# A power of two numbers per partition, moved behind a large sum on GpSimd, in the layers of an attention and feed-forward kernel

## The chip, the cores and the metric

The kernel runs on one core of a Trainium2 chip. A core has five engines, each with a queue of its own that it works off strictly in order: TensorE (PE; its weight loads are listed apart as PEld), VectorE (DVE), ScalarE (ACT), GpSimd (POOL) and SyncE (SP), which here only starts DMAs. Engines wait for one another by semaphores. The metric is the device time of one execution in microseconds; the kernel before took 2054.12 us, the median of three runs (2053.56 to 2055.71).

## The reference

`x` is (1, 2048, 128) in float32. It first goes through an RWKV block with a layer norm, then through six layers of local attention and a gated feed-forward, and a last layer norm. The change lies in the six layers:

```
for i in range(6):
    x = attn_layer(shift_tokens(x), Wqkv[i], ...) + x      # 16 heads of 64, window 32
    x = ffn_layer(shift_tokens(x), ln_g[i], ln_b[i], ...) + x

attn_layer:  q, k, v = split(x @ Wqkv);  q = l2norm(q) * qs;  k = l2norm(k) * ksc
             q = q*cos*scale + rotate_half(q)*sin*scale;  k = k*cos/scale + rotate_half(k)*sin/scale
             out = softmax(8 * q k^T in the window) v;  return out @ Wo
ffn_layer:   mu = mean(x);  var = mean((x-mu)^2);  xn = (x-mu)/sqrt(var + 1e-5) * g + b
             a, gate = split(xn @ W1 + b1);  return a * gelu(gate) @ W2 + b2
```

The power in question is `(var + eps) ** -0.5` of the feed-forward's norm.

## The kernel before

`layers` works in 96 steps of one tile of 128 tokens, 16 tiles in each of six layers, as a software pipeline. In step `s` each engine does a slice of several tiles: the projection, norm and rotation of tile `p = s + 1`, the scores of tile `a = s`, the softmax's rest and the output of tile `b = s - 1`, and, of a pair of tiles some steps back, a slice of the feed-forward. The norm of the feed-forward (`norm`) and its second product (`down`) lie in the odd steps, the first product (`up`) in the even ones. The code is written out by hand for every engine, and that order is the order of the queue. Steps -1 to 6 are unrolled, 88 steps run in a loop of two (an odd one, then an even one), the rest is unrolled again.

The names that matter here:

- `unit[0]`, `unit[1]`: q and k divided by their norms, by DVE, L1152. The inverse root is made by nine small DVE instructions in a chain (`inverse_root`, L88 to L104) from `sums`. All nine read and write SBUF; of them L88, L90, L92, L94 begin the chain. L88 waits for nothing but the sums and its place in the queue behind `heads_out` (L1133), which takes the product of probabilities and values (PE, L1290) out of PSUM.
- POOL's queue for tile `p`: `turns` (the rotary tables of this tile, L993), in odd steps `shift_f` (L1001, L1002), then `shift_a` of the tile after (two copies, L962 and L963), then the first `across` pair (L974, waits for `unit[0]`), `along[0]` (L1008), `rotated[0]` (L982), the second `across` pair (L974, of k), and `rotated[1]` (L982, in `add_turned(1, p)`). `along[1]` is made by DVE (L1210).
- `rotated[1] = along[1] + across[1]`, 128 x 1024 elements, is what PE transposes as `turn<-identity,rotated` in the following step (the second of the two groups at L1223 there). `add_turned` waits for POOL's own `across` through the semaphore `acrossed`, and for DVE's `along[1]`.
- `rstd_f = var_f ** -0.5`, 128 x 2 elements, POOL, L1016. DVE writes `var_f` (L1204) right ahead of its `along[1]`. ACT reads `rstd_f` in the following step, behind its copies to `k_t`, for `rstd_diag` (L1074).
- `proj_a<-w_qkv,shift_a` at L1328: PE's projection of v. It waits for `unit[0]`, since both use the PSUM bank `proj_a`.

Of the kernel before, what the change touches and what calls it, by code (L numbers as in the profile page):

```python
# [65 lines left out]
def after(engine, semaphore, count):  # L66

    if not isinstance(count, int) or count > 0:
        engine.wait_ge(semaphore, count)
# [38 lines left out]
def tile_of(n):  # L108
    return n % TILES


def layer_of(n):
    return n // TILES


def columns(n, count=1):

    return bass.ds(tile_of(n) * TILE + 1, TILE * count)


def columns_before(n, count=1):

    return bass.ds(tile_of(n) * TILE, TILE * count)
# [667 lines left out]
def layers(nc, ctx, given):  # L791
# [12 lines left out]
    with ExitStack() as own:  # L804
# [76 lines left out]
        def halves(buffer):  # L881
            return buffer[:, :, :].rearrange("p h (two e) -> p h two e", two=2)
# [10 lines left out]
        def run(engine, step):  # L893


            for s in range(-1, FIRST):
                step(s, (s - 5) // 2 if s % 2 else (s - 6) // 2, s % 2, alive(s))
            with engine.Fori(0, ROUNDS) as i:
                step(i * 2 + FIRST, i + 1, 1, alive(FIRST + 2))
                step(i * 2 + FIRST + 1, i + 1, 0, alive(FIRST + 3))  # L900
            for s in range(FIRST + 2 * ROUNDS, STEPS + 4):
                step(s, (s - 5) // 2 if s % 2 else (s - 6) // 2, s % 2, alive(s))

        with nc.Block() as block:
# [49 lines left out]
            @block.gpsimd  # L954
            def _(pool):
                pool.wait_ge(tables_in, 48)

                def shift_input(m, odd, pairs_done):

                    after(pool, v_projected, 2 * (m - 1))  # L960
                    pool.wait_ge(xa_ready, XA_BASE + pairs_done)
                    pool.tensor_copy(shift_a[odd][0:64, :], xa[0:64, columns(m)]).then_inc(shifted, 1)  # L962
                    pool.tensor_copy(shift_a[odd][64:128, :], xa[64:128, columns_before(m)]).then_inc(shifted, 1)  # L963
                    pool.wait_ge(shifted, 2 * m + 2)

                def cross(j, p, odd):

                    pool.wait_ge(united[j], p + 1)
                    after(pool, rotated_in[j], p)
                    u, a = halves(unit[j]), halves(across[j])  # L970
                    for half in range(2):
                        table = turns[odd][:, 2 * j + 1, 32 * half:32 * half + 32].unsqueeze(1).broadcast_to(
                            [128, HEADS, 32])
                        pool.tensor_tensor(a[:, :, 1 - half, :], u[:, :, half, :], table, ALU.mult)\  # L974
                            .then_inc(acrossed[j], 1)

                def add_turned(j, p):

                    pool.wait_ge(alonged[j], p + 1)
                    pool.wait_ge(acrossed[j], 2 * p + 2)  # L980
                    after(pool, (q_turned, k_turned)[j], 2 * p)
                    pool.tensor_tensor(rotated[j][:, :, :], along[j][:, :, :], across[j][:, :, :],  # L982
                                       ALU.add).then_inc(rotated_in[j], 1)

                shift_input(0, 0, -XA_BASE + 1)

                def step(s, h, odd, live):
                    p, mine = s + 1, 1 - odd
                    if live["p"]:
                        after(pool, alonged[1], p - 1)  # L990
                        after(pool, acrossed[1], 2 * (p - 1))
                        after(pool, alonged[0], p - 1)
                        pool.tensor_tensor(turns[mine][:, :, :], where[:, tile_of(p), :, :], scales[:, layer_of(p), :, :],  # L993
                                           ALU.mult).then_inc(table_made, 1)
                        pool.wait_ge(table_made, p + 1)
                    if live["norm"]:
                        pool.wait_ge(xb_ready, s - 1)
                        after(pool, dev_made, h + 1)
                        after(pool, rotated_in[1], p if live["p"] else STEPS)
                        after(pool, rstd_made, h + 1)  # L1000
                        pool.tensor_copy(shift_f[0:64, :], xb[0:64, columns(s - 3, 2)]).then_inc(f_shifted, 1)  # L1001
                        pool.tensor_copy(shift_f[64:128, :], xb[64:128, columns_before(s - 3, 2)]).then_inc(f_shifted, 1)  # L1002
                        pool.wait_ge(f_shifted, 2 * (h + 2))
                    if live["next"]:
                        shift_input(s + 2, odd, h - 4 if odd else h - 3)
                    if live["p"]:
                        cross(0, p, mine)
                        pool.tensor_tensor(along[0][:, :, :], unit[0][:, :, :],  # L1008
                                           turns[mine][:, 0, :].unsqueeze(1).broadcast_to([128, HEADS, HEAD]),
                                           ALU.mult).then_inc(alonged[0], 1)  # L1010
                        add_turned(0, p)
                        cross(1, p, mine)
                    if live["norm"]:
                        pool.wait_ge(var_kept, h + 2)
                        after(pool, rstd_laid, 2 * (h + 1))
                        pool.tensor_tensor(rstd_f[:, :], var_f[:, :], minus_half[:, 0:2], ALU.pow).then_inc(rstd_made, 1)  # L1016
                    if live["p"]:
                        add_turned(1, p)

                run(pool, step)  # L1020

            @block.scalar
# [505 lines left out]
```

## Time and profile before

| | us |
|---|---|
| median of 3 runs | 2054.12 |
| profiled execution, its own time | 2057.84 |
| its span | 2056.0 |
| PE busy in the span | 1815.7 (88%) |
| DVE busy | 1577.9 (77%) |
| POOL busy | 1480.3 (72%) |
| ACT busy | 1163.3 (57%) |

Busy time says how full a queue is, not which queue the others wait for. No engine is full, and four of them work on each step in turn, so the order in time of single instructions has to be read: who starts right after whom, in every step again. The layers take the span from about 250 us to about 2030 us.

### The profile page before, as it was taken

The page shows a single profiled execution, that of the slowest core. Times are in us where ns is not written, and L with a number is a line of the kernel's source. Part 1 is how long each engine was busy: PE and PEld are TensorE (multiplying, and loading weights), DVE is VectorE, ACT ScalarE, POOL GpSimd, SP SyncE. Part 2 cuts the span into 40 slices and gives each one's busy share as a digit, 9 for nine tenths or more (in the row PEclk, how much of TensorE's full clock was granted, in tenths as well). Part 3 has the DMA queues.
Part 4 walks back from the last instruction along what each step waited for, and adds up shares of the span by engine and source line. Part 5 has one row for each costly group of instructions (what it writes and reads, how often), then busy time and mean ns, then how long its engine had stood idle before and what let it go on. Part 6 is the DMA issues. An engine that isn't in the chain of part 4 may idle for free. (4 is left out here: it accounts for less than half of the span.)

```text
span 2056.0 us, 85960 instructions
## 1 busy us (share of the span) xinstructions
PE 1815.7 (88%) x34280; PEld 1319.2 (64%) x34280; DVE 1577.9 (77%) x2776; ACT 1163.3 (57%) x1966; POOL 1480.3 (72%) x1159
## 2 busy tenths in 40 slices
PE   7765489999999999999999999999999999999985
PEld 3445256676766666666666666666666666666664
DVE  3455578888888888887888888888888888888864
ACT  2211155666656656666566666666666666666662
POOL 2221478878888788887888877878788787887871
PEclk9776699999999999999999999999999999999997
DMA  4000022222322223222223222223222232222220
GB/s 147 2 2 2 21 63 64 57 53 77 81 67 58 53 58 92 68 65 53 60 61 87 56 72 61 61 54 86 71 65 60 53 85 68 72 58 53 54 61 21
DMA packets 93581, 123.43 MB, mean 60 GB/s; under 512 B 27760, under 2 KB 41808, under 8 KB 93392
## 3 DMA queue, kind: packets, MB, share of 16 engines
q1 hardware_dynamic: 93232, 122.42, 23.7%
q8 instruction: 46, 0.75, 0.2%
q10 hardware_dynamic: 288, 0.13, 0.0%
q14 instruction: 15, 0.12, 0.0%
HBM read 20.74 MB, written 1.05 MB: 11 GB/s over the span
## 5 line engine op out<-in xcount | busy, mean ns | idle before, releaser
L974 POOL TENSOR_TENSOR across<-unit,turns 128x512 f32<-128x512 f32 x384 | 524.7, 1386 | 266.5 <-issue 254.9
L982 POOL TENSOR_TENSOR rotated<-along,across 128x1024 f32<-128x1024 f32 x192 | 495.7, 2582 | 20.4 <-POOL along L1008 9.7
L1127 DVE TENSOR_REDUCE sums<-squares 128x16 f32<-128x1024 f32 x192 | 234.2, 1220 | 157.2 <-ACT squares L1030 151.1
L1223 PE MATMUL turn<-identity,rotated 128*128 128x128 f32 x1536 | 205.1, 277 | 56.2 <-POOL rotated L982 56.2
L1223 PEld LDWEIGHTS turn<-identity,rotated 128*128 128x128 f32 x1536 | 172.5, 141 | 118.7 <-issue 101.7
L1008 POOL TENSOR_TENSOR along<-unit,turns 128x1024 f32<-128x1024 f32 x96 | 227.4, 2369 | 0.0
L1328 PE MATMUL proj_a<-w_qkv,shift_a 128*128 128x512 f32 x384 | 190.2, 618 | 35.0 <-DVE unit L1152 25.0
L1089 ACT COPY val<-proj_a 128x1024 f32<-128x1024 f32 x96 | 97.2, 1012 | 180.2 <-PE proj_a L1328 180.2
L1353 PEld LDWEIGHTS att<-o_t,w_o 128*128 128x128 f32 x1536 | 188.0, 193 | 6.1 <-issue 1.0
L1065 ACT COPY k_t<-turn 128x512 f32<-128x512 f32 x192 | 103.3, 589 | 154.3 <-PE turn L1223 154.3
L1353 PE MATMUL att<-o_t,w_o 128*128 128x128 f32 x1536 | 188.3, 276 | 0.0
L1256 PE MATMUL proj_a<-w_qkv,shift_a 128*128 128x512 f32 x384 | 183.6, 601 | 4.3 <-POOL shift_a L962 3.0
L1210 DVE TENSOR_TENSOR along<-unit,turns 128x1024 f32<-128x1024 f32 x96 | 183.1, 1908 | 0.0
L1271 PE MATMUL proj_b<-w_qkv,shift_a 128*128 128x512 f32 x384 | 181.2, 594 | 0.0
L1030 ACT ACTIVATE squares<-proj_a 128x1024 f32<-128x1024 f32 x96 | 98.2, 1023 | 114.2 <-PE proj_a L1256 114.2
L1316 PEld LDWEIGHTS turn<-k_t,q_t 64*32 64x32 f32 x12288 | 128.7, 105 | 41.9 <-issue 41.5
L1290 PE MATMUL att<-v_win,p_t 64*32 64x64 f32 x12288 | 153.6, 225 | 0.8 <-ACT p_t L1050 0.8
L1050 ACT COPY p_t<-att 128x512 f32<-128x512 f32 x192 | 103.2, 589 | 89.6 <-PE att L1223 89.6
L1290 PEld LDWEIGHTS att<-v_win,p_t 64*32 64x32 f32 x12288 | 135.5, 105 | 19.5 <-issue 16.9
L1133 DVE TENSOR_TENSOR heads_out<-att,inv_mass 128x512 f32<-128x512 f32 x192 | 123.7, 686 | 29.7 <-PE att L1290 29.7
L1316 PE MATMUL turn<-k_t,q_t 64*32 64x64 f32 x12288 | 144.6, 226 | 0.0
L1144 DVE TENSOR_TENSOR logits<-turn,row_max 128x512 f32<-128x512 f32 x192 | 132.8, 692 | 6.7
(203 smaller groups left out, 3468.9 us busy)
## 6 DMA issues: line engine op xcount, KB each, us to landing
v_win<-val SPq DMA_DIRECT2D x1536, 64.0 KB, 2.0
w_qkv<-wqkv_dram SPq DMA_DIRECT2D x18, 512.0 KB, 3.9
w_o<-wo_dram SPq DMA_DIRECT2D x6, 512.0 KB, 4.6
where<-positions_dram SPq DMA_DIRECT2D x1, 2048.0 KB, 11.5
w_ffn<-ffn_dram SPq DMA_DIRECT2D x12, 170.5 KB, 2.3
w_ffn<-ffn_dram SPq DMA_DIRECT2D x6, 192.0 KB, 2.3
x_tok<-x_dram SPq DMA_DIRECT2D x4, 256.0 KB, 4.3
out_dram<-final SPq DMA_DIRECT2D x4, 256.0 KB, 2.4
```

Of the source, the lines that this page charges most:

```text
L974: pool.tensor_tensor(a[:, :, 1 - half, :], u[:, :, half, :], table, ALU.mult)\
L982: pool.tensor_tensor(rotated[j][:, :, :], along[j][:, :, :], across[j][:, :, :], ALU.add).then_inc(rotated_in[j], 1)
L1008: pool.tensor_tensor(along[0][:, :, :], unit[0][:, :, :], turns[mine][:, 0, :].unsqueeze(1).broadcast_to([128, HEADS, HEAD]), ALU.mult).th ...
L1127: dve.tensor_reduce(sums[:, j, :], squares[j][:, :, :], AX.X, ALU.add).then_inc(summed[j], 1)
L1210: dve.tensor_tensor(along[1][:, :, :], unit[1][:, :, :], turns[mine][:, 2, :].unsqueeze(1).broadcast_to([128, HEADS, HEAD]), ALU.mult).the ...
L1223: mm = pe.transpose(bank[:, TILE * (i % 4):TILE * (i % 4) + TILE], buffer[:, TILE * i:TILE * i + TILE], identity[:, :])
L1256: mm = pe.matmul(bank_a[:, half, :], shift_a[mine][:, :], w_qkv[:, 512 * half:512 * half + 512], start=True, stop=True)
L1271: mm = pe.matmul(bank_b[:, half, :], shift_a[mine][:, :], w_qkv[:, base:base + 512], start=True, stop=True)
L1290: mm = pe.matmul(bank_s[WINDOW * w:WINDOW * w + WINDOW, par, HEAD * a_:HEAD * a_ + HEAD], p_t[rows, a_, WINDOW * w:WINDOW * w + WINDOW], v ...
L1316: mm = pe.matmul(bank_t[WINDOW * w:WINDOW * w + WINDOW, par, HEAD * a_:HEAD * a_ + HEAD], q_t[rows, a_, WINDOW * w:WINDOW * w + WINDOW], k ...
L1328: pe.matmul(bank_a[:, par, :].rearrange("p (a e) -> p a e", a=PAIRS), shift_a[mine][:, :], values[:, par, :, :], start=True, stop=True).th ...
L1353: mm = pe.matmul(bank_s[:, 0, 0:TILE], w_o[:, a_, :], o_t[:, a_, :], start=(a_ == 0), stop=(a_ == PAIRS - 1))
```

## The change

In POOL's `step`, the power (L1016 before, L1018 after) and the sum `add_turned(1, p)` change places. The waits of each go with it. Nothing else is changed, and the queues of PE, DVE, ACT and SP stay as they are.

```diff
                         add_turned(0, p)
                         cross(1, p, mine)
+                    if live["p"]:
+                        add_turned(1, p)
                     if live["norm"]:
                         pool.wait_ge(var_kept, h + 2)
                         after(pool, rstd_laid, 2 * (h + 1))
                         pool.tensor_tensor(rstd_f[:, :], var_f[:, :], minus_half[:, 0:2], ALU.pow).then_inc(rstd_made, 1)
-                    if live["p"]:
-                        add_turned(1, p)
```

POOL's queue at the end of the odd step in the loop, and the start of the even step behind it (the difference; ISA and REGISTER_ALU are the sequencer's own small instructions):

```order
 L982 TENSOR_TENSOR rotated<-along,across 128x1024
 L974 TENSOR_TENSOR across<-unit,turns 128x16x32 x2
+L982 TENSOR_TENSOR rotated<-along,across 128x1024
 L69 REGISTER_ALU
-L1016 TENSOR_TENSOR rstd_f<-var_f,minus_half 128x2
-L982 TENSOR_TENSOR rotated<-along,across 128x1024
+L1018 TENSOR_TENSOR rstd_f<-var_f,minus_half 128x2
 L993 ISA
```

The second `across` pair was followed by the power and is now followed by the sum; ahead of `turns` (L993) of the next step now stands the power.

The same place in the unrolled steps 3 and 5, at the end of the odd step:

```order
 L982 TENSOR_TENSOR rotated<-along,across 128x1024
 L974 TENSOR_TENSOR across<-unit,turns 128x16x32 x2
-L1016 TENSOR_TENSOR rstd_f<-var_f,minus_half 128x2
 L982 TENSOR_TENSOR rotated<-along,across 128x1024
+L1018 TENSOR_TENSOR rstd_f<-var_f,minus_half 128x2
 L993 TENSOR_TENSOR turns<-where,scales 128x256
 L962 COPY shift_a<-xa 64x128
```

The two instructions have changed places here as well. The last two powers of the 48 lie in steps that have no rotation left; there nothing moves.

## Rows read from the trace of the kernel before

**Rows 1.** Stretches: us, busy us (and instructions) of each engine, PEclk, DMA share, GB/s.

```profile
265.00:1944.00 1679.00, 1563.14 (x30231) 1150.22 (x30229) 1379.39 (x2362) 1053.88 (x1764) 1357.88 (x1048) 1.00 0.26 65
1008.28:1026.38 18.10, 16.70 (x330) 12.35 (x330) 15.15 (x26) 9.52 (x18) 14.86 (x11) 1.00 0.24 58
```

**Rows 2.** Waits of PE: who waited for whom, us in total, times, longest.

```profile
PE turn L1223 <- POOL rotated L982: 56.2, 51, 3.8
PE proj_a L1328 <- DVE unit L1152: 25.0, 49, 0.6
```

**Rows 3.** Timeline of PE and PEld: start us, us, what, [idle before <- releaser].

```profile
1008.34 0.30 PEld L1328 LDWEIGHTS proj_a<-w_qkv,shift_a 128*128 128x128 f32 x2 [0.71 <-issue]
...
1022.36 1.09 PE L1223 MATMUL turn<-identity,rotated 128*128 128x128 f32 x8 [0.99 <-POOL rotated L982]
...
1026.45 0.30 PEld L1328 LDWEIGHTS proj_a<-w_qkv,shift_a 128*128 128x128 f32 x2 [0.23 <-issue]
```

**Rows 4.** Timeline of DVE, the `unit` before and the chain at 1021 to 1026.

```profile
1007.05 1.23 DVE L1152 TENSOR_TENSOR unit<-proj_a,inv_norm 128x1024 f32<-128x1024 f32 x1
...
1021.56 1.29 DVE L1133 TENSOR_TENSOR heads_out<-att,inv_mass 128x512 f32<-128x512 f32 x2 [0.27 <-PE att L1290]
1022.76 0.20 DVE L88 SCALAR_TENSOR_TENSOR sums_min<-sums 128x32 f32<-128x32 f32 x1
...
1023.23 0.32 DVE L92 TENSOR_TENSOR root_work<-inv_norm 128x32 f32<-128x32 f32 x1
1023.58 0.31 DVE L94 TENSOR_TENSOR root_work<-root_work,sums_min 128x32 f32<-128x32 f32 x1
...
1025.15 1.23 DVE L1152 TENSOR_TENSOR unit<-proj_a,inv_norm 128x1024 f32<-128x1024 f32 x1
```

**Rows 5.** Timeline of POOL, end of odd step 41 and start of step 42.

```profile
1015.75 3.48 POOL L974 TENSOR_TENSOR across<-unit,turns 128x512 f32<-128x512 f32 x2
1019.19 0.71 POOL L1016 TENSOR_TENSOR rstd_f<-var_f,minus_half 128x2 f32<-128x2 f32 x1
1019.87 2.36 POOL L982 TENSOR_TENSOR rotated<-along,across 128x1024 f32<-128x1024 f32 x1
1022.19 0.73 POOL L993 TENSOR_TENSOR turns<-where,scales 128x256 f32 x1
1023.22 0.28 POOL L962 COPY shift_a<-xa 64x128 f32 x1 [0.30 <-POOL turns L993]
1023.56 0.29 POOL L963 COPY shift_a<-xa 64x128 f32 x1
```

**Rows 6.** Timeline of POOL, end of even step 40, which has no power.

```profile
997.73 2.49 POOL L974 TENSOR_TENSOR across<-unit,turns 128x512 f32<-128x512 f32 x2
1000.36 2.37 POOL L982 TENSOR_TENSOR rotated<-along,across 128x1024 f32<-128x1024 f32 x1
1002.69 0.72 POOL L993 TENSOR_TENSOR turns<-where,scales 128x256 f32 x1
```

**Rows 7.** Timeline of DVE: the chain's first instruction at 271 us.

```profile
271.47 0.18 DVE L88 SCALAR_TENSOR_TENSOR sums_min<-sums 128x32 f32<-128x32 f32 x1
271.69 0.19 DVE L90 SCALAR_TENSOR_TENSOR inv_norm<-sums_min,magic 128x32 int32<-128x32 int32 x1
```

**Rows 8.** Timeline of POOL behind step 3.

```profile
322.96 0.73 POOL L993 TENSOR_TENSOR turns<-where,scales 128x256 f32<-128x256 f32 x1
323.76 0.28 POOL L962 COPY shift_a<-xa 64x128 f32<-64x128 f32 x1
```

**Rows 9.** Timeline of DVE behind step 3.

```profile
323.00 0.74 DVE L88 SCALAR_TENSOR_TENSOR sums_min<-sums 128x32 f32<-128x32 f32 x1
323.78 0.31 DVE L90 SCALAR_TENSOR_TENSOR inv_norm<-sums_min,magic 128x32 int32<-128x32 int32 x1
```

**Rows 10.** Timeline of POOL behind step 93, the last one.

```profile
1980.81 0.73 POOL L993 TENSOR_TENSOR turns<-where,scales 128x256 f32 x1
```

**Rows 11.** Timeline of DVE behind step 93.

```profile
1981.36 0.23 DVE L88 SCALAR_TENSOR_TENSOR sums_min<-sums 128x32 f32<-128x32 f32 x1
```

**Rows 12.** Timeline of ACT at 1023 us.

```profile
1023.05 1.07 ACT L1065 COPY k_t<-turn 128x512 f32<-128x512 f32 x2 [2.06 <-PE turn L1223]
1024.01 0.70 ACT L1074 ACTIVATE rstd_diag<-identity,rstd_f 128x128 f32<-128x128 f32 x2
```

**Rows 13.** Groups by line, POOL: count, busy us, mean ns, idle before.

```profile
L1016 POOL TENSOR_TENSOR rstd_f<-var_f,minus_half 128x2 f32<-128x2 f32 x48 | 33.7, 703 | 15.8 <-issue 15.8
```

## The prediction

> **What bounds the kernel now.** I read the waits of PE first, because PE is the fullest engine. The longest wait in it is for `rotated` from POOL, 56.2 us in 51 waits; the second is that of the v projection for `unit`, 25.0 us in 49 [rows 2]. The change makes `rotated[1]` earlier in just the steps of which the first wait speaks, so it looks like a gain of up to 0.5 us each. The timeline says whether that is worth anything. The stretch 265 to 1944 us runs at the full granted clock (1.00, 2.4 GHz) [rows 1], so no step there is bent by the clock, and the steps repeat: I took one pair, steps 41 and 42, as the sample.
>
> In it PE waits 0.99 us for `rotated`, transposes from 1022.36, and starts the v projection at 1026.45 [rows 3]. DVE's `unit[0]` ends at 1025.15 + 1.23 = 1026.38 [rows 4], 0.07 ahead of that start. In the step before, `unit[0]` ends at 1007.05 + 1.23 = 1008.28 [rows 4] and the v projection starts at 1008.34 [rows 3], again 0.06 to 0.07 behind it, although PE had been idle for 0.71 us there and for 0.23 us here [rows 3]. Whatever slack PE has, it starts when `unit[0]` is done. So the end of `unit[0]` paces both steps, and PE's wait for `rotated` lies inside time that PE would otherwise idle away a few microseconds later.
>
> What paces `unit[0]`: PE is occupied from the v projection on until the product of probabilities and values, then DVE takes over. `heads_out` begins 0.27 us after that product [rows 4], and then the chain runs without a break, `heads_out` 1.29, the nine small instructions of the root, `unit[0]` 1.23. One step is 1026.38 - 1008.28 = 18.10 us [rows 1, 4]: some 13 us PE, some 5 us DVE. Neither part waits for `rotated[1]`.
>
> But the root chain is not DVE's alone. Left alone, L88 takes 0.18 and its successors 0.19 us [rows 7]. Behind step 3, L88 takes 0.74 and ends at 323.74; POOL's `turns` ends at 322.96 + 0.73 = 323.69. L90 then takes 0.31 and ends at 324.09; POOL's first `shift_a` ends at 323.76 + 0.28 = 324.04 [rows 8, 9]. Each time the DVE instruction lasts until 0.05 us after the POOL instruction beside it. In the sample L88 ends at 1022.96, `turns` at 1022.92; L92 takes 0.32 and ends at 1023.55, the first copy at 1023.50; L94 takes 0.31 and ends at 1023.89, the second copy at 1023.85 [rows 4, 5]. Behind step 93 it is 1981.59 against 1981.54 [rows 10, 11]. Between the first and the last, steps 5 to 91, there are 44 more steps with the power, all with this distance. So in each odd step the end of `turns`, which is the end of POOL's whole queue for a tile, already sets the end of L88, and with it `unit[0]`. POOL's queue and the PE-DVE loop are level to within a few hundredths there.
>
> A rule of the Trainium skill bears on this (SBUF — State Buffer, Who interferes with whom): a DVE instruction with two SBUF inputs and a GpSimd instruction that reads SBUF exclude each other for a whole instruction, and the one issued first goes first. The trace agrees: 0.74 against 0.18 us. By a mild slowdown instead of exclusion, L88 would have ended near 323.2 in step 3.
>
> **The change part by part.** It removes nothing and adds nothing; all durations stay. Two instructions of POOL change places in 46 odd steps that have both (48 powers [rows 13], less the two in steps without rotation).
>
> *The sum.* Its wait for `across` was covered by the power. In the sample the second `across` pair ends at 1015.75 + 3.48 = 1019.23, the power starts at 1019.19 and the sum at 1019.87 [rows 5], without a gap. Where there is no power, the pair ends at 997.73 + 2.49 = 1000.22 and the sum starts at 1000.36 [rows 6], 0.14 later, the time for POOL's own semaphore to come round. That gap now appears in the odd steps too.
>
> *The end of POOL's queue.* Counted from the end of the pair: before, `turns` starts at 1022.19 - 1019.23 = 2.96. Now the sum starts at 0.14, the power 2.32 later (1022.19 - 1019.87, [rows 5]; 2.33 in [rows 6]), and `turns` 0.68 after the power (1019.87 - 1019.19). That is 3.14. `turns` starts 0.18 later. The queue holds the same work and has got 0.18 us longer: 0.14 of gap, and 0.04 because the power used to start that much ahead of the pair's end.
>
> *What that costs.* `turns` at 1022.37 to 1023.10 still lies over the start of L88 (1022.76), so L88 ends at 1023.15 instead of 1022.96. The first `shift_a` keeps its 0.30 us behind `turns`, the second follows; L92 and L94 meet them as before, all 0.18 later. `unit[0]` ends 0.18 later, and so does the step. 46 x 0.18 = 8.3 us.
>
> *Bounds of that term.* The step from the power to `turns` isn't in the trace. The power was followed by the sum with an overlap of 0.03; two small copies follow one another with a gap of 0.06 (1023.56 against 1023.50) [rows 5]. With the gap `turns` comes 0.27 later, 12.4 us in all. From below: were the sum's wait already met, as behind the power, the queue would be as long as before, 0. Below nothing it can't come by this term, as no work leaves the queue. I take 0.18, which is put together from neighbours in the same queue.
>
> *What is gained.* `rotated[1]` ends 0.68 - 0.18 = 0.50 earlier and PE's wait of 0.99 shrinks by as much. The transposes of `heads_out` behind it wait for DVE until 1022.85 in any case [rows 4]. PE comes to its v projection up to 0.5 earlier and waits there for `unit[0]`: 0, covered by DVE's chain.
>
> *The power itself, later.* It ends at 1019.23 + 0.14 + 2.32 + 0.71 = 1022.40. ACT uses it at 1024.01, behind the copies to `k_t` that begin at 1023.05 [rows 12]; these may begin 0.5 earlier, ACT then asks at 1023.51. Margin 1.1 us, cost 0. The power now lies beside `heads_out` (1021.56 to 1022.85), which reads PSUM and has kept its 1.29 beside `rotated` too [rows 4, 5], and ends before L88 begins. Cost 0. Behind the power in the queue now stand only `turns` and the copies; `var_f` is older by some microseconds, so its wait isn't felt.
>
> The other rule (GPSIMD Engine Reference, Instruction dispatch): the end of an instruction gates whoever waits on its semaphore, but doesn't hold back the next GpSimd instruction. The trace agrees: 0.04 ahead of the end without a wait, 0.14 behind it with one. It speaks against the change, since it makes a short instruction that waits for nothing recent the filler of exactly that gap; were the two orders equal in length, the sum would be 0.
>
> **Against the median.** The profiled execution took 2057.84 (span 2056.0 and 1.8 around it), 3.7 over the median of the runs. The steps are so regular that I add the 8.3 to the median: 2054.1 + 8.3 = 2062.4 us. About 0.2%, 4.1 us, is what a measurement of this kernel can tell from no change.
>
> **The rivals.**
>
> *It does nothing.* The gap is lost in POOL's idle time before the first `across` (it waits for `unit[0]`) and L88 is not carried along, because its closeness to `turns` is chance. For it: L88 is stretched by only 0.02 to 0.05 in the loop. Against it: step 3's 0.74, and L88's end never precedes that of `turns` there. 2054.1 us.
>
> *It gets faster: L92 slips out from between the copies.* If `turns` does not hold L88, the chain keeps its place at 1022.76 while the copies come 0.18 later; L92 then needs 0.19 or meets only the first copy, and L94 ends with the first copy (1023.68 + 0.05) instead of with the second (1023.89): 0.16 less per step, 46 x 0.16 = 7.4, so 2046.7. The decisive point is whether L88 is held by `turns`. The larger form of the same side is PE's wait paid out in full: 46 x 0.5 = 23 us, 2031. It would need a v projection that starts without `unit[0]`; [rows 3, 4] speak against it in both steps.
>
> *It gets slower by more.* The gap of the copies, or a further wait that the sequencer pays once the short power stands right ahead of `turns`: `shift_a` must be late by the same amount, and L96 behind L94 would stay free. 0.27 a step, 2066.5.
>
> **How the numbers follow.** The forecast, with 0.14 to 0.22 a step, has 0.66; slower by more 0.08; nothing 0.18; faster 0.08. The likeliest case's own range is 2060.5 to 2064.5 (46 x 0.14 to 46 x 0.22). Holding 8 in 10 takes it and part of the two neighbours: from 2054.0 to 2065.5. Slower by over 0.2% (above 2058.2) is 0.66 + 0.08, and 0.01 from the upper end of nothing: 0.75; same 0.17; faster 0.08.
>
> **What would show it.** In the profile after: the sum starts 0.13 to 0.14 behind the second `across` pair; `turns` starts 3.14 after the pair's end instead of 2.96; L88 grows from 0.20 to 0.38 in the even steps and still ends 0.05 after `turns`; L92 and L94 stay at 0.32 and 0.31; the span from one `unit[0]` to the next grows from 18.10 to 18.28 across an odd-even border and stays in the other; PE's wait for `rotated` falls from 56 to about 33 us, while the idle time before the v projection grows by as much and more. I am wrong if L88 ends before `turns`, if the sum's gap does not appear, or if the v projection starts without regard to `unit[0]`.

## The result, and the profile after

| | before | after |
|---|---|---|
| median, six runs each | 2055.2 us | 2064.72 us |
| range of the runs | 2053.56 to 2057.18 | 2058.42 to 2066.68 |
| ratio, 95% interval | | 1.0041 (1.0025 to 1.0057) |
| span of the profiled execution | 2056.0 | 2064.1 |

The changed kernel is 0.4% slower. Applied to the 2055.2 us the ratio is 8.4 us, where 8.3 was forecast. Its interval reaches from 5 to 12 us, and the plain difference of the medians is 9.5 us, so the agreement to 0.1 us is closer than the runs can tell and is partly luck. The runs of the changed kernel scatter over 8 us, and the scatter goes with the granted clock: 0.965 in the run of 2058.42, 0.957 in that of 2066.68. In the profiled executions of both kernels the stretch from 265 to 1944 us, the layers, shows the full granted clock (1.00), so I put the scatter down to the block ahead of them and to the end. The other executions have no profile, so this isn't shown for each of them. For that reason the experiments below are read in two ways, by the ratio and by the time between two instructions inside the layers.

First POOL in the changed kernel, at the end of step 41 and the start of 42. A row gives the start, the length in us, the instruction and, in brackets, the idle time before it with what ended it. It answers to [rows 5]:

```profile
1020.67 3.48 POOL L974 TENSOR_TENSOR across<-unit,turns 128x512 f32<-128x512 f32 x2
1024.28 2.37 POOL L982 TENSOR_TENSOR rotated<-along,across 128x1024 f32<-128x1024 f32 x1
1026.61 0.71 POOL L1018 TENSOR_TENSOR rstd_f<-var_f,minus_half 128x2 f32<-128x2 f32 x1
1027.29 0.73 POOL L993 TENSOR_TENSOR turns<-where,scales 128x256 f32 x1
1028.31 0.28 POOL L962 COPY shift_a<-xa 64x128 f32 x1 [0.30 <-POOL turns L993]
1028.65 0.29 POOL L963 COPY shift_a<-xa 64x128 f32 x1
```

The second `across` pair ends at 1024.15. The sum starts 0.13 behind it, where the power had started 0.04 ahead of it; the power follows at 2.46, `turns` at 3.14. In [rows 5] `turns` stood at 2.96. The durations are those of before.

The same steps on DVE, against [rows 4]:

```profile
1026.46 1.29 DVE L1133 TENSOR_TENSOR heads_out<-att,inv_mass 128x512 f32<-128x512 f32 x2 [0.26 <-PE att L1290]
1027.67 0.40 DVE L88 SCALAR_TENSOR_TENSOR sums_min<-sums 128x32 f32<-128x32 f32 x1
1028.10 0.19 DVE L90 SCALAR_TENSOR_TENSOR inv_norm<-sums_min,magic 128x32 int32<-128x32 int32 x1
1028.33 0.32 DVE L92 TENSOR_TENSOR root_work<-inv_norm 128x32 f32<-128x32 f32 x1
1028.68 0.31 DVE L94 TENSOR_TENSOR root_work<-root_work,sums_min 128x32 f32<-128x32 f32 x1
...
1030.24 1.23 DVE L1152 TENSOR_TENSOR unit<-proj_a,inv_norm 128x1024 f32<-128x1024 f32 x1
```

L88 has grown from 0.20 to 0.40 and ends at 1028.07, 0.05 behind `turns` (1028.02). The instructions behind it have their old lengths. From the start of L88 to the start of `unit[0]` it was 2.39 us (1025.15 - 1022.76) and is 2.57.

PE in the same steps, with its weight loads (PEld), against [rows 3]:

```profile
1026.78 1.09 PE L1223 MATMUL turn<-identity,rotated 128*128 128x128 f32 x8 [0.48 <-POOL rotated L982]
...
1031.57 0.67 PE L1328 MATMUL proj_a<-w_qkv,shift_a 128*128 128x512 f32 x1 [0.77 <-DVE unit L1152]
```

```profile
1031.54 0.30 PEld L1328 LDWEIGHTS proj_a<-w_qkv,shift_a 128*128 128x128 f32 x2 [0.90 <-issue]
```

PE waits 0.48 for `rotated` instead of 0.99, and 0.90 instead of 0.23 ahead of the v projection. Its weight loads for that projection start 0.07 behind the end of `unit[0]` (1031.47), as before. The waits of PE, summed over the whole execution (us in total, times, longest), against [rows 2]:

```profile
PE proj_a L1328 <- DVE unit L1152: 60.0, 92, 0.8
PE turn L1223 <- POOL rotated L982: 33.0, 51, 3.8
```

The wait that the eye falls on first has shrunk by 23.2 us and the kernel has become slower. The other has grown by 35.0: it has taken up the 23 us and the 8 of the later `unit[0]`. The rest of about 4 us is no new wait: PE waited some 0.1 us in each step behind the power before as well, which the view mostly didn't count (49 times, now 92).

Over the layers: `unit[0]` of tile 0 and of tile 93 in the kernel before, and then in the one after.

```profile
236.50 1.22 DVE L1152 TENSOR_TENSOR unit<-proj_a,inv_norm 128x1024 f32<-128x1024 f32 x1
...
1946.91 1.23 DVE L1152 TENSOR_TENSOR unit<-proj_a,inv_norm 128x1024 f32<-128x1024 f32 x1
```

```profile
238.07 1.22 DVE L1152 TENSOR_TENSOR unit<-proj_a,inv_norm 128x1024 f32<-128x1024 f32 x1
...
1956.40 1.23 DVE L1152 TENSOR_TENSOR unit<-proj_a,inv_norm 128x1024 f32<-128x1024 f32 x1
```

That is 1710.4 and 1718.3 us, 7.9 more over the 45 steps with the power that lie between: 0.176 each. I call this distance the layers' time. It leaves out what happens ahead of the layers (the first `unit[0]` comes 1.6 us later) and at the end (1.4 us shorter). It is read from the one profiled execution of each kernel, so it has no interval of its own. Of the 7.9 us, 7.6 lie in the steps behind the power and 0.3 in the others.

### The profile page after: what moved, and what is told of

It reads as the page before. It is cut to its first block and busy times, and to the rows that moved or that the text cites. A ratio compares the mean times of both kernels' runs of the same rounds, so it can differ in the third digit from the quotient of the medians.

```text
span 2064.1 us, 85960 instructions
## 1 busy us (share of the span) xinstructions
PE 1818.0 (88%) x34280; PEld 1318.7 (64%) x34280; DVE 1584.7 (77%) x2776; ACT 1162.7 (56%) x1966; POOL 1482.4 (72%) x1159
## 5 line engine op out<-in xcount | busy, mean ns | idle before, releaser
L1030 ACT ACTIVATE squares<-proj_a 128x1024 f32<-128x1024 f32 x96 | 98.2, 1023 | 114.3 <-PE proj_a L1256 114.3
L1328 PEld LDWEIGHTS proj_a<-w_qkv,shift_a 128*128 128x128 f32 x384 | 65.9, 191 | 126.5 <-issue 126.4
```

The source lines that it names most:

```text
L1328: pe.matmul(bank_a[:, par, :].rearrange("p (a e) -> p a e", a=PAIRS), shift_a[mine][:, :], values[:, par, :, :], start=True, stop=True).th ...
```

## The experiments

In all that follows, "held" means that a DVE instruction of the root chain, which alone takes 0.18 or 0.19 us, lasts until 0.05 us after the end of the POOL instruction beside it; the `chain` is the time from the start of L88 to the start of `unit[0]`.

The theory: DVE's root chain is held by `turns` and the copies of `shift_a` on POOL, so the end of POOL's queue reaches `unit[0]`; the exchange made that queue 0.18 us longer, because it uncovered the sum's wait for `across`. The rivals: the loss comes from the power being late or standing right ahead of `turns`; the length of POOL's queue sets the pace without any hold; the order of sum and power costs by itself; PE is the bound once `rotated` is early.

All in one table, the traces read as above. The ratio is to runs of the kernel before made beside the kernel in question: median 2055.2 us for the changed kernel, 2056.7 for two_powers and turns_late_before, 2057.21 for the other four. The chain is given as its median in the steps behind the power, and in the others.

| kernel | median us | ratio (95%) | layers' time | chain |
|---|---|---|---|---|
| before | 2055.2 to 2057.21 | 1 | 1710.4 | 2.39 / 2.33 |
| after | 2064.72 | 1.0041 (1.0025 to 1.0057) | 1718.3 | 2.57 / 2.33 |
| power_inside | 2064.11 | 1.0031 (1.0019 to 1.0043) | 1718.4 | 2.57 / 2.34 |
| power_idle | 2047.50 | 0.9951 (0.9938 to 0.9964) | 1704.8 | 2.33 / 2.27 |
| two_powers | 2069.08 | 1.0058 (1.0039 to 1.0076) | 1725.3 | 2.79 / 2.21 |
| turns_late_before | 2038.48 | 0.9916 (0.9899 to 0.9933) | 1697.6 | 2.16 / 2.12 |
| turns_late_after | 2037.46 | 0.9902 (0.9888 to 0.9917) | 1694.0 | 2.21 / 2.12 |
| turns_late_power_idle | 2030.05 | 0.9868 (0.9852 to 0.9884) | 1689.1 | 2.12 / 2.12 |

In the steps behind the power, L88 starts 15.72 or 15.73 us (median) after the start of the `unit[0]` of the tile before, in every one of the eight kernels. In the other steps it is 16.42 to 16.44, but for turns_late_before with 16.59. So the part ahead of the chain, PE's, is untouched, and the chain carries the difference.

The hold can be counted over the eight traces, which have 6912 instructions of the chain. If each is expected to end when its own 0.18 or 0.19 us are over, or 0.05 us after the end of the POOL instruction (other than a power) that was running when it began, whichever is later, 6879 end within 0.03 us of that. The other 33 began within 0.02 us of a copy; they kept their own length, and the copy took longer instead.

The cuts of the code below are shortened, with `...` for what is left out. They are against the changed kernel where nothing else is said.

**power_inside: the power without a gap to fill.**

```diff
 def cross(j, p, odd, power=None):
     for half in range(2):
         pool.tensor_tensor(a[:, :, 1 - half, :], u[:, :, half, :], table, ALU.mult).then_inc(acrossed[j], 1)
+        if half == 0 and power is not None:
+            power()                       # in odd steps, for j == 1
...
-    if live["norm"]: ... ALU.pow ...      # no longer behind the sum
```

> The power stands between the two across instructions of k in the odd steps, so it fills no gap and both it and the sum's wait for across are paid. The gap theory: the end of POOL's queue (turns) comes 3.14 us after where the pair would have ended alone, as in the changed kernel, L88 is held by turns for about 0.38 us, and a pair of steps takes 0.18 us longer than in the kernel before: about 2062 to 2064 us. PE's wait for rotated grows instead of shrinking (rotated[1] ends 0.18 later than before, its idle time about 1.17 instead of 0.99). The rival, that the loss comes from the later power or from the power right ahead of turns: the power is earlier than before here and turns follows the sum, so the time is that of the kernel before, 2055.

POOL, DVE and PE's sum of waits:

```profile
1020.62 1.28 POOL L974 TENSOR_TENSOR across<-unit,turns 128x512 f32<-128x512 f32 x1
1022.03 2.36 POOL L984 TENSOR_TENSOR rotated<-along,across 128x1024 f32<-128x1024 f32 x1
1024.35 0.73 POOL L1001 TENSOR_TENSOR turns<-where,scales 128x256 f32 x1
```

```profile
1024.76 0.36 DVE L88 SCALAR_TENSOR_TENSOR sums_min<-sums 128x32 f32<-128x32 f32 x1
```

```profile
PE turn L1229 <- POOL rotated L984: 64.6, 51, 3.8
```

The median of 2064.1 is at the upper edge of what was expected, the interval of the ratio overlaps that of the changed kernel, and the layers' time is the same to 0.1 us. `turns` ends at 1025.08 and L88 at 1025.12; behind it come the same 0.19, 0.32, 0.31 as in the changed kernel. PE's wait for `rotated` is 64.6 us, 8.4 more than in [rows 2], where the changed kernel has 23.2 less. Two kernels with `rotated[1]` early and late, and with the power late and early, cost the same. So neither the place of the power nor the readiness of `rotated` decides. What they share is the uncovered gap: in both the sum starts 0.13 behind `across`. The rival of the late power has fallen, and so has that of the power right ahead of `turns`.

**power_idle: the power out of the queue's tight part.**

```diff
     if live["next"]:
         shift_input(s + 2, odd, h - 4 if odd else h - 3)
+    if live["up"]:                        # even steps; waits for var_kept and rstd_laid as before
+        pool.tensor_tensor(rstd_f[:, :], var_f[:, :], minus_half[:, 0:2], ALU.pow).then_inc(rstd_made, 1)
...
-    if live["norm"]: ... ALU.pow ...
```

> The power stands in the even steps behind the copies of shift_a, in POOL's idle time ahead of the first across. POOL's queue up to turns is 0.49 us shorter than before (2.47 instead of 2.96 after the pair). The hold theory: turns ends 0.3 us before L88 begins and holds nothing, but the two copies at +0.30 and +0.64 behind it now hold L88 and L90 instead of L92 and L94, so the chain ends only 0.03 us earlier than before: 2053 to 2055 us, 0.4% under the changed kernel, no more. A plain queue-length theory, in which the end of turns alone sets the pace, would give 0.49 us a pair of steps back against before: 2033. The rival that the late power costs: slower than the changed kernel, since it is later still by 1.3 us (ACT's rstd_diag would wait 0.1 to 0.5 us).

DVE behind the shorter queue:

```profile
1017.87 0.26 DVE L88 SCALAR_TENSOR_TENSOR sums_min<-sums 128x32 f32<-128x32 f32 x1
1018.16 0.31 DVE L90 SCALAR_TENSOR_TENSOR inv_norm<-sums_min,magic 128x32 int32<-128x32 int32 x1
1018.50 0.19 DVE L92 TENSOR_TENSOR root_work<-inv_norm 128x32 f32<-128x32 f32 x1
```

and POOL beside it:

```profile
1016.77 0.72 POOL L993 TENSOR_TENSOR turns<-where,scales 128x256 f32 x1
1017.79 0.28 POOL L962 COPY shift_a<-xa 64x128 f32 x1 [0.30 <-POOL turns L993]
1018.13 0.29 POOL L963 COPY shift_a<-xa 64x128 f32 x1
```

`turns` ends at 1017.49, 0.38 ahead of L88, and is harmless. But the two copies now meet L88 and L90: 0.26 and 0.31 us, each ending 0.05 after its copy, and L92 is free. The queue is 0.50 us shorter than before (`turns` starts 2.46 behind the pair, median) and the chain only 0.06 (median), against 0.03 expected. So the queue's length alone is not the pace; what lies over what counts. The power is later than in any other kernel, and here ACT does wait for it, for 47 of the 48 powers and 0.63 us in the median, a little more than the 0.1 to 0.5 named for it (total, times, longest):

```profile
ACT rstd_diag L1074 <- POOL rstd_f L1009: 30.5, 47, 1.7
```

In the kernels before and after there is one such wait, of 1.7 us. The 47 waits aren't paid: L88 still starts 15.72 us behind the `unit[0]` before it, and the kernel is faster. The total was misjudged: 2053 to 2055 was expected and 2047.5 measured. Of that the layers' time explains 5.6 us: 3.3 in the steps behind the power and 2.2 in the others, where L92 was held in 30 of 44 steps instead of 38, and for a shorter time (chain 2.27 instead of 2.33), which I had not reckoned with. Of the rest, the two profiled executions show 2.2 us ahead of the layers and 1.7 behind the last `unit[0]` compared; what of that is scatter and what the change is not shown.

**two_powers: the queue made longer still.**

```diff
     pool.tensor_tensor(rstd_f[:, :], var_f[:, :], minus_half[:, 0:2], ALU.pow).then_inc(rstd_made, 1)
+    pool.tensor_tensor(spare[:, :], ones[:, 0:2], minus_half[:, 0:2], ALU.pow).then_inc(spared, 1)
```

> The changed kernel with a second power (of ones, into a tile that nothing reads) behind the first in the odd steps, so POOL's queue is another 0.68 us longer and turns comes at 3.81 after the pair instead of 3.13. Hold theory: turns now begins after L88, so L88 (0.18) and L90 (0.19) are free and L92 is held by turns to its end (about 0.6), L94 is free, and L96 and L98 meet the two copies (0.3 each) if these start first: the chain from L88 to unit grows from 2.57 to about 2.8 us, a third of what was added; 2064 plus 46 x 0.24, about 2075 (2066 to 2078). If the length of POOL's queue set the pace by itself, all 0.68 would be paid: 2096. If nothing but the gap mattered and the queue's end did not: 2064.

POOL, then DVE:

```profile
1031.26 0.69 POOL L1022 TENSOR_TENSOR spare<-ones,minus_half 128x2 f32<-128x2 f32 x1
1031.92 0.72 POOL L995 TENSOR_TENSOR turns<-where,scales 128x256 f32 x1
1032.95 0.28 POOL L964 COPY shift_a<-xa 64x128 f32 x1 [0.30 <-POOL turns L995]
1033.29 0.29 POOL L965 COPY shift_a<-xa 64x128 f32 x1
```

```profile
1031.63 0.18 DVE L88 SCALAR_TENSOR_TENSOR sums_min<-sums 128x32 f32<-128x32 f32 x1
1031.84 0.19 DVE L90 SCALAR_TENSOR_TENSOR inv_norm<-sums_min,magic 128x32 int32<-128x32 int32 x1
1032.07 0.63 DVE L92 TENSOR_TENSOR root_work<-inv_norm 128x32 f32<-128x32 f32 x1
1032.73 0.19 DVE L94 TENSOR_TENSOR root_work<-root_work,sums_min 128x32 f32<-128x32 f32 x1
1032.96 0.32 DVE L96 SCALAR_TENSOR_TENSOR root_work<-root_work 128x32 f32<-128x32 f32 x1
1033.31 0.31 DVE L98 SCALAR_TENSOR_TENSOR inv_norm<-root_work,inv_norm 128x32 f32<-128x32 f32 x1
```

The hold has moved two instructions down: L92 lasts to the end of `turns` (1032.65 + 0.05), L96 and L98 to the ends of the copies. The chain is 2.79 us, as worked out; 0.68 us more of queue cost 0.22 there. The total, 2069, lies below the 2075 named as the likeliest. In the layers' time the steps behind the power cost 10.2 us more than in the changed kernel, and the other steps 3.1 less, as their chain got shorter (2.21 in the median instead of 2.33); the rest is within the scatter of these runs (2062 to 2074). One of the other steps shows how:

```profile
1014.17 0.34 POOL L964 COPY shift_a<-xa 64x128 f32 x1 [0.38 <-POOL shift_f L1005]
```

```profile
1014.17 0.19 DVE L92 TENSOR_TENSOR root_work<-inv_norm 128x32 f32<-128x32 f32 x1
```

Both start at the same hundredth. L92 keeps its 0.19, and it is the copy that takes 0.34 instead of 0.28. Whichever is first is not held. That only a third of the added length is paid is against the rival in which the queue's length alone sets the pace (2096).

**turns_late_after: `turns` taken from beside the chain.**

```diff
-    if live["p"]: ... turns ...           # ahead of the copies
     if live["next"]:
+        after(pool, rotated_in[1], p)
+        if live["up"]: pool.wait_ge(rstd_made, h + 2)
         shift_input(s + 2, odd, h - 4 if odd else h - 3)
+    if live["p"]:
+        pool.wait_ge(rooted, ROOT_OPS * p + ROOT_OPS)
+        ... turns ..., pool.wait_ge(table_made, p + 1)
```

The edit also makes the copies wait for POOL's own sum and power ahead of them.

> The changed kernel, with turns behind the copies of shift_a and held back until the root chain is done (a wait for the ninth instruction), so that it runs beside unit, which reads PSUM. Hold theory: L88 to L94 meet at most the copies; in even steps the second copy holds L90 until about 0.22 us earlier than the chain before, in odd steps nothing holds L92 and L94 (0.20 us gained). Against before 0.4 us a pair, against the changed kernel 0.6: about 2036 to 2040. If PE, not unit, set the pace once rotated is earlier: no gain against before. If holding were a matter of the length of POOL's queue, no gain or a loss, since turns comes later than ever.

POOL, with `turns` behind the copies and the chain:

```profile
1015.98 0.28 POOL L962 COPY shift_a<-xa 64x128 f32 x1 [0.36 <-issue]
1016.32 0.29 POOL L963 COPY shift_a<-xa 64x128 f32 x1
1018.56 0.73 POOL L1007 TENSOR_TENSOR turns<-where,scales 128x256 f32 x1 [1.94 <-DVE inv_norm L104]
```

20 us less than before, 27 less than the changed kernel; the layers' time falls by 16.4 and 24.3. This undoes the loss of the change without touching the order of power and sum, by making `turns` later. So the loss doesn't come from anything that waits for `turns` to be ready. Expected were 0.22 and 0.20 us per step, measured 0.18 (steps of 18.11 and now 17.93 us, medians) and 0.19 (18.75 and 18.56). The part in the steps behind the power is smaller because the copies, 0.36 us behind the power, still lie over the chain: L92 is held in 33 of 45 of these steps (0.28), L88 and L90 in 11.

**turns_late_before: the same, with the order of before.** The diff is the same against the kernel before, without the wait for `rstd_made`.

> The kernel before (power ahead of the sum), with turns behind the copies and held until the root chain is done. Without the hold by turns DVE's chain would end 0.17 us earlier in the steps with the power and 0.20 in the others. But rotated[1] ends as late as before there, and PE had only 0.23 us ahead of its v projection, of which about 0.1 is its own changeover: PE may set the pace at 0.14. So 46 x (0.14 to 0.17 + 0.20): 2039 to 2042, at most 3 us behind turns_late_after. If the order of power and sum were a loss in itself, whatever turns does, this kernel would be 8 us ahead of turns_late_after: 2029.

It stands 1.0 us behind turns_late_after in the median. The two were run beside different sets of the kernel before, so the ratios count, 0.9916 and 0.9902, and their intervals overlap. So once `turns` is out of the way the order of the change costs nothing: the order is no loss in itself. In the layers' time turns_late_after is even 3.6 us ahead. That is a difference of two parts: it gains 7.0 us where PE would otherwise come late, as expected, and loses 3.4 in the chain, where its later copies lie over L88 to L92. It also has one wait more (for `rstd_made`), so the two kernels differ by a little more than the order. PE's weight loads in turns_late_before:

```profile
1016.15 1.32 PEld L1318 LDWEIGHTS turn<-k_t,q_t 64*32 64x32 f32 x128 [0.42 <-issue]
1017.62 0.30 PEld L1330 LDWEIGHTS proj_a<-w_qkv,shift_a 128*128 128x128 f32 x2
```

`unit[0]` ends at 1017.41 there, and PE starts the v projection 0.21 later, straight behind its scores; the median in the steps behind the power is 0.22, where it is 0.07 in the seven other kernels. This is the one kernel in which PE and not `unit[0]` sets that start, and so the one in which an earlier `rotated` would be worth time.

**turns_late_power_idle: both.** The diff is that of turns_late_before with the power moved as in power_idle.

> As turns_late_after, but the power stands in the even steps behind the copies of shift_a and ahead of the held turns. Hold theory: both copies end before L88 begins (1022.5 in the sample's time), only the power lies beside L88; a power reads two elements of each partition, so it holds L88 for between 0 and 0.6 us. Without a hold 0.31 in even steps and 0.20 in odd steps: 2030 to 2034, the fastest of the four; with the full hold 2050 to 2058.

POOL, then DVE:

```profile
1009.80 0.71 POOL L1003 TENSOR_TENSOR rstd_f<-var_f,minus_half 128x2 f32<-128x2 f32 x1 [0.17 <-POOL shift_a L963]
1012.04 0.73 POOL L1009 TENSOR_TENSOR turns<-where,scales 128x256 f32 x1 [1.54 <-DVE inv_norm L104]
```

```profile
1009.73 0.18 DVE L88 SCALAR_TENSOR_TENSOR sums_min<-sums 128x32 f32<-128x32 f32 x1
1009.95 0.19 DVE L90 SCALAR_TENSOR_TENSOR inv_norm<-sums_min,magic 128x32 int32<-128x32 int32 x1
1010.17 0.19 DVE L92 TENSOR_TENSOR root_work<-inv_norm 128x32 f32<-128x32 f32 x1
```

The power runs beside L90 and L92 and neither is stretched. In the median all nine instructions have their free length in both kinds of step, and the chain is 2.12 us. This is the fastest kernel: 0.9868 of before, 27 us.

## Why the prediction was right

- *What bounds the kernel.* The end of `unit[0]`, held at its start by `turns`. Right: the v projection follows `unit[0]` by 0.07 us in the kernels before and after, and taking `turns` away makes both kinds of step shorter.
- *The gap.* Forecast 0.14 us between `across` and the sum, measured 0.13. `along[1]`, the other thing that the sum waits for, was done 2.36 us ahead of the pair's end (median), so the gap is the wait for `across`; `turns` at 3.14 after the pair, measured 3.14 in the sample (3.13 as the median). power_inside shows that it is this gap and not the places of the two instructions.
- *The step.* Forecast 18.28 us across an odd-even border and no change in the other step; the medians went from 18.11 to 18.29 and from 18.75 to 18.76.
- *The hold.* L88 was forecast at 0.38 and took 0.40 in the sample, 0.38 as the median. The weakest point of the argument was that the loop showed a stretch of only 0.02 to 0.05 us, and that one step (0.74 us) had to carry the rule. two_powers and power_idle moved the hold to other instructions of the chain, each where the start times put it. By its wording, one of the prediction's signs of being wrong came up once in 46 times: behind step 3 of the changed kernel L88 ends 0.70 us before `turns`. There `turns` started behind L88 and held L90 instead, for 0.72 us, so that step didn't get longer (chain 2.82 before, 2.78 after). The mechanism is the same, but it doesn't always take L88.
- *The sum.* 46 x 0.18 = 8.3 us; by the ratio 8.4, in the layers' time 7.9 over 45 steps. The range of the likeliest case was added up a little too wide: 46 x 0.22 gives 2064.2, not 2064.5, which changes nothing.
- *The gain of 0.5 us for PE.* Taken at nothing and worth nothing: 23.2 us off one wait, 35.0 on the next. turns_late_before shows the case in which PE has no slack: there its lateness costs 7.0 us in the layers' time, about 0.15 a pair of steps.
- *The later power.* Taken at nothing, and ACT waits for it no more than before (once, 1.7 us). In power_idle it is later still; ACT then waits 30.5 us for it in all, and even that isn't paid.
- *The rivals.* That L88 is not carried along was given 0.18 and was wrong, as were the faster case and that of the larger loss: `turns` came 0.17 later (median), not 0.27.

## What to carry to other kernels

An instruction that waits for nothing recent is worth its place between a producer and a consumer on the same engine: there it fills the 0.13 us of waiting for the engine's own semaphore, and behind both it doesn't. An engine with 28% idle time can still set the pace, if its last instructions before a pause lie over a chain of short instructions of another engine that it holds; look for a short instruction whose length varies and whose end follows another engine's by a constant. Where such a pair is found, move the long one away from the chain instead of shaving the queue: beside `unit[0]`, which reads PSUM, it held nothing here (`unit[0]` kept its 1.23 us). That gave 18 to 20 us, the shorter queue alone 10, and both together 27.

## What the runs showed of the hardware

The hold acts in both directions and for whichever comes second: a copy that started together with L92 took 0.34 us instead of 0.28, and L92 its free 0.19. With such a tie, hundredths of a microsecond elsewhere can shift 0.1 us per step (the other steps of two_powers). What is held doesn't start over when it is let go: L88 takes 0.18 us alone, but ends 0.05 us after `turns`. So where L88 meets only the last 0.16 us of `turns`, it costs 0.02 us [rows 4, 5].

The power doesn't hold. It takes 0.71 us and reads two SBUF operands, and L90 and L92 beside it took 0.19 each in turns_late_power_idle. Over the eight traces 415 instructions of the chain overlap a power and no other POOL instruction, and none is stretched by more than 0.01 us. The Trainium skill (SBUF — State Buffer, Who interferes with whom) would have a GpSimd instruction that reads SBUF exclude such a DVE instruction; for `turns` and the copies the trace agrees, for an instruction of two elements per partition it doesn't show it. Whether that is due to its size or to its being a power was not tested.
